# Reordering the pipelined steps of a gated-trace and attention kernel: out matmuls two lags ahead, moments two products ahead, three table steps earlier

## What is computed

```python
# block 1
ctx = causal_ema(x, tau_ctx)
gated = x * sigmoid(concat([x, ctx]) @ Wg.T + bg)
mod = 0.5 + sigmoid(gelu(x @ Wn1.T + bn1) @ Wn2.T + bn2)          # 32 channels
traces = [causal_ema(gated * mod[d], tau_raws[d]) for d in range(32)]
temporal = einsum('dbtc,dc->btc', traces, softmax(blend, axis=0))
gate = sigmoid(temporal @ Wtemp.T + btemp)
out = (gelu(x @ Wsoma.T + bsoma) * gate) @ Wout.T
x = x + (out - mean(out)) / sqrt(var(out) + 1e-5) * gamma + beta
# block 2: attention with 16 heads of 8; each row of the batch takes either the dense
# softmax with a prior bias, or the sparse one over 32 gathered neighbours, by its lam
Q, K, V = x @ Wq.T + bq, x @ Wk.T + bk, x @ Wv.T + bv
x = x + attention(Q, K, V, prior_mask, prior_indices, lam) @ Wo.T + bo
```

## Time and profile before

| what | us |
|---|---|
| median of 3 runs | 333.78 |
| lowest and highest of them | 333.19, 334.94 |
| the profiled execution, its own time | 332.17 |
| its span in the profile | 330.4 |

### The profile page before, as it was taken

How to read it: one execution, slowest core, us unless ns; L and a number is a source line. 1 busy time by engine, 2 the same in 40 slices (tenths; PEclk the granted TensorE clock), 3 DMA queues, 4 the chain that set the end, 5 groups by cost and what they waited for, 6 DMA issues and landing times. The chain is left out here.

```text
span 330.4 us, 9991 instructions
## 1 busy us (share of the span) xinstructions
PE 308.8 (93%) x3319; PEld 209.8 (64%) x3335; DVE 275.5 (83%) x1453; ACT 214.8 (65%) x458; POOL 246.6 (75%) x298
## 2 busy tenths in 40 slices
PE   8997888999999999999978898999999999999995
PEld 2554554746557375655535666878788778877873
DVE  3988898888969887796889666999999999999972
ACT  6763155555656646566446678778887887788863
POOL 3263586678686875665456966999999999999990
PEclk9999999999999999999999999999999999999999
DMA  6600021050412305013530435564444354301011
GB/s 187 211 2 26 7 67 32 16 129 3 111 34 59 86 0 145 1 35 66 77 51 2 82 94 86 82 133 127 129 102 117 87 129 100 72 7 30 5 34 32
DMA packets 29154, 23.07 MB, mean 70 GB/s; under 512 B 2736, under 2 KB 27824, under 8 KB 29104
## 3 DMA queue, kind: packets, MB, share of 16 engines
q1 hardware_dynamic: 29104, 22.44, 29.1%
HBM read 7.75 MB, written 2.10 MB: 30 GB/s over the span
## 5 line engine op out<-in xcount | busy, mean ns | idle before, releaser
L1596 POOL TENSOR_TENSOR arena<-arena,neg_max 128x512 f32<-128x512 f32 x128 | 129.6, 1042 | 14.1 <-DVE neg_max L1438 13.9
L1438 DVE CUSTOM_DVE_ANT_0 arena<-ps,arena 128x128 f32<-128x128 f32 x512 | 113.5, 286 | 11.5 <-PE ps L762 5.9
L1077 ACT ACTIVATE arena<-ps 128x512 f32<-128x512 f32 x128 | 69.6, 597 | 9.0 <-PE ps L776 9.0
L776 PE MATMUL ps<-ident_sb,arena 128*128 128x128 f32 x512 | 68.2, 276 | 0.0
L776 PEld LDWEIGHTS ps<-ident_sb,arena 128*128 128x128 f32 x512 | 56.4, 141 | 7.0 <-issue 4.3
L1515 POOL TENSOR_TENSOR arena<-arena 128x448 f32<-128x448 f32 (+6 forms) x56 | 42.8, 764 | 23.1 <-DVE arena L1269 19.7
L1438 DVE DVE_READ_ACCUMULATOR2_ANT neg_max<- 128x1 f32 x512 | 42.4, 83 | 0.0
L792 PE MATMUL ps<-arena 128*32 128x128 f32 x1024 | 41.2, 279 | 0.0
L1502 POOL TENSOR_TENSOR arena<-decay_a,arena 128x192 f32<-128x192 f32 x32 | 19.4, 636 | 21.8 <-ACT arena L921 21.8
L1269 DVE SCALAR_TENSOR_TENSOR arena<-ps,lag_c,arena 128x448 f32<-128x448 f32 (+6 forms) x56 | 25.7, 483 | 7.7 <-POOL arena L1515 7.0
L792 PEld LDWEIGHTS ps<-arena 128*32 128x32 f32 x1024 | 24.1, 109 | 6.9 <-issue 0.3
(11 more groups left out here) (169 smaller groups left out, 581.9 us busy)
## 6 DMA issues: line engine op xcount, KB each, us to landing
arena<-q_parts SPq DMA_DIRECT2D x96, 64.0 KB
arena<-k_parts SPq DMA_DIRECT2D x96, 64.0 KB
arena<-in_x SPq DMA_DIRECT2D x16, 256.0 KB, 3.4
arena<-in_xt SPq DMA_DIRECT2D x8, 256.0 KB, 2.8
out<-arena SPq DMA_DIRECT2D x7, 256.0 KB, 3.0
arena<-in_consts SPq DMA_DIRECT2D x1, 420.0 KB, 4.0
w_sb<-in_w SPq DMA_DIRECT2D x1, 384.0 KB, 6.2
w_sb<-in_w SPq DMA_DIRECT2D x1, 192.0 KB, 4.4
```

Of the source, the lines that this page charges most:

```text
L776: mm = pe.transpose(ps[1][:, q % 2, k * P:k * P + P], neg_t[q % NT_RING][:, k * P:k * P + P], ident)
L1077: act.activation(probT[q % PT_RING], ps[1][:, q % 2, :], ACT.Exp, scale=-1.0)\
L1438: dve.tensor_tensor_reduce(out=neg_t[q % NT_RING][:, cs], in0=ps[0][:, score_bank(c) + slot, cs], in1=nbias[n % 2], scale=1.0, scalar=3.0e ...
L1596: pool.tensor_tensor(t4, t4, neg_max[:, n % 2, 4 * z:4 * z + 4].unsqueeze(2).broadcast_to([P, 4, P]), ALU.subtract).then_inc(s["shifted"], 1)
```

## The change

Four things are moved; nothing is computed otherwise and no instruction is added or dropped.

1. On PE `b_out` (and the `c_less` ahead of it) stands behind lag 5 in place of lag 6, in all steps, and lags 6 and 7 come between `b_out` and `c_v`. Before, only lag 7 came behind `b_out`, and behind `c_v`.
2. On DVE `c_moments` stands behind product 5 in place of product 6, and products 6 and 7 come between it and `c_centre`. On POOL `c_rstd` moves the same way, ahead of the additions of lags 6 and 7.
3. `neighbours` goes from step 0, where it stood ahead of `c_moments`, to the end of `front`.
4. In step 0 `kept_bias` on DVE goes from ahead of `c_moments` to ahead of `b_temporal`, and `value_bias` on PE from behind `b_gate` to ahead of `b_cross`.

The core of the diff:

```diff
@@ tensor: step @@
                     f_gate_ctx(i, m + 1)
+                    value_bias()
                     b_cross(i, m)
...
                 b_gate(i, m)
-                if not closes:
-                    value_bias()
                 if closes:
                     c_less(i, m - 1, 1, 1)
                     c_less(i, m - 1, 0, 0)
-                f_lags(i, m + 1, range(4, 7))
+                f_lags(i, m + 1, range(4, 6))
                 if closes:
                     c_less(i, m - 1, 0, 1)
                 b_out(i, m)
+                f_lags(i, m + 1, range(6, Q))
                 if closes:
                     c_v(i, m - 1)
-                f_lags(i, m + 1, range(7, Q))
@@ vector: front and step @@
                 b_carries(i, m, NJ - 1, NJ)
+                neighbours()
...
+                if not closes:
+                    dve.wait_ge(s["const_ps"], 2)
+                    dve.wait_ge(s["rows_loaded"], 16)
+                    pro("kept_bias", dve.tensor_tensor(kept_bias[:], bank(1, 3)[:, 0:P], bo, ALU.add), waited=False)
                 b_temporal(i, m)
...
                 b_mixed(i, m)
-                f_lags(i, m + 1, range(4, 7))
-                if not closes:
-                    dve.wait_ge(s["const_ps"], 2)
-                    dve.wait_ge(s["rows_loaded"], 16)
-                    pro("kept_bias", dve.tensor_tensor(kept_bias[:], bank(1, 3)[:, 0:P], bo, ALU.add), waited=False)
-                    neighbours()
+                f_lags(i, m + 1, range(4, 6))
                 c_moments(i, m)
-                f_lags(i, m + 1, range(7, Q))
+                f_lags(i, m + 1, range(6, Q))
                 c_centre(i, m)
```

## The result

The changed kernel took 330.54 us (median of 10 runs, 329.62 to 331.27), the kernel before 333.12 (median of 10, 332.25 to 334.94; the three runs shown first had given 333.78). The ratio is 0.9919, with a 95% interval of 0.9901 to 0.9937: 2.6 us faster. I had forecast 332.1 and a range of 331.0 to 333.6. The direction was right, the size was not: the gain was 2.6 in place of 1.65. (One of six later executions of the changed kernel had a granted clock of about 0.75 from start to end and took 387.52 us; no table here uses it.)

The account below looks back on a forecast made before the run. In steps 2 to 5 PE and ACT set the pace; in step 1 DVE was late. The terms 1.2 + 0.15 + 0.3 = 1.65 us off 333.78 gave 332.1 us, range 331.0 to 333.6.

Parts of the forecast that it names:

- The blocks: Octet steps behind the pipeline: they keep their order, so a microsecond gained at the start is one at the end.
- The neighbour steps and the key bias at no cost: Front and step 0: 1.0 us and 0.28 us on DVE land in its pauses and cost nothing.
- a sign of being wrong: Step 0: an L572 that comes later than 30.1 us would show the prediction wrong.
- Step 0, out and moments: End of step 0: `b_out` and DVE's statistics start earlier, so the carries' product begins 1.21 us earlier.
- What is late next in step 1: Step 1, DVE's split of the modulation meeting POOL on the shared port: `b_cross` gains 1.2 us, ends 0.95 and 1.35.
- my rival of collisions: POOL wins the port and holds L1251, later steps lose 0.05 each: gain 1.0 us, 332.8 us, chance 0.13.
- Steps 1 to 5: Out and lags: the values' copy holds the carries, so 0.03 us a step, 0.15 for five; ends -0.1 and +0.2 a step.
- my sign of being wrong: Steps 2 to 5: a period that moves by 0.1 us or more either way would show the prediction wrong.
- Step 6: Copy of the values behind ACT's logarithm: it starts 0.3 us earlier and the gain passes on.
- The rival that the later steps gain too: If the copy's wait does not hold the carries, each later step gains: 2.6 us in all, 331.1 us, chance 0.12.
- The slower rival: PE's fp32 and bf16 changes cost about 0.24 us each, delaying `c_v` in six steps: 335.0 us, chance 0.08.
- The base: Whole kernel: the gain of 1.65 us was subtracted from a median of 333.78 us.

Follow-up runs that it names:

- the first four: Tables alone, reordering alone, PE's new order with tables, vector engines' new order with tables, against the kernel before: 0.62, 1.82, 2.43 and 0.18 us ahead.
- the next three: Changed kernel with two more matmuls ahead of `c_v` (0.01 us behind before), `c_v` ahead of both lags (4.20 ahead), POOL's beta addition earlier (step 1 18.74 us).
- both edits: Changed kernel with `c_v` ahead of both lags on PE and POOL's beta addition ahead of the inverse deviation: median 328.42 us, ratio to before 0.9859.
- the late-values kernel: Changed kernel with two more bf16 matmuls on PE between the lags and `c_v`: step period 19.75 us, 0.01 us behind the kernel before.
- `c_v` first: Changed kernel with `c_v` ahead of both lags on PE: 4.20 us ahead of the kernel before, ratio to it 0.9882.

## Why the prediction was wrong, point by point

The sum was 1.2 + 0.15 + 0.3 = 1.65, and the traces have 0.84 + 1.26 + 0.50 = 2.60. The term that failed is that of steps 1 to 5, 0.03 a step where 0.25 was measured.

- **The blocks.** Right: what the pipeline won moved the octet steps as a block, apart from the disturbances (shortest spans 2.6 apart, pipeline 2.60). The other kernels' shortest spans say the same, each 330.4 less its "ahead" to 0.1 us: 329.8, 328.6, 328.0 and 330.2 for the first four, 330.4, 326.3 and 327.2 for the next three, 325.6 for both edits.
- **The neighbour steps and the key bias at no cost.** Right. DVE's pause ahead of group 0's locals shrank from 1.33 to 0.59 us, and `b_cross` of step 0 did not wait longer for them: the PE pause ahead of it is 0.29 in place of 0.51. It stands at 30.45, past the 30.1 that I had named as a sign of being wrong, but so does everything in this execution; in the nine other traces with the tables in front it is at 30.11 to 30.15, in the two without at 30.10 and 30.14.
- **Step 0, out and moments: 1.21.** Nearly right. From `b_out`'s first matmul (37.57) to the statistics it was 1.17, not 1.09, and the carries' product was 1.10 earlier (41.92 less the 0.35 of this execution, against 42.67).
- **What is late next in step 1: 1.2, with 0.95 and 1.35 as ends.** Wrong by 0.36, and outside its ends. The mechanism stood as I wrote it, the size didn't: L1531 came 0.77 us earlier, not 1.04. Of the 0.27, 0.11 is the inverse deviation (1.36 earlier, not 1.47), the rest the addition of lag 6 behind it, which cost 0.60, not 0.43. And POOL won the second meeting (46.13 against 46.31), the half of my rival of collisions that came true; its other half, a loss in the later steps, didn't. In all twelve traces with the full clock in the pipeline L1245 (L1246 before) of step 1 ends 0.54 to 0.56 us behind POOL's L1531, though its row is between 1.27 and 1.75 long, while POOL's row keeps its 1.26 or 1.27. The 0.79 of step 2, which I took for the free time, is such a row too: it ends 0.54 behind POOL's 62.95 + 1.28; the late-values kernel has four steps without a meeting, and there the row takes 0.69. It goes the other way as well: the second instruction of POOL's L1501, at 46.69 beside L1250, took 1.04 where the others took 0.59 or 0.60. The Trainium skill (SBUF — State Buffer, "SBUF: two separate sides") calls the shared port an exclusive lock; these rows agree. I had used the rule for a sentence; with POOL's one addition out of the way the step got 0.65 shorter.
- **Steps 1 to 5: 0.03 a step.** The step that failed most: 0.25 a step, 1.26 in all in place of 0.15. The reasoning (the copy holds the carries, so count to `c_v`, not to `b_out`) was right; the kernels with `c_v` later and `c_v` first show it. The term was a difference of two sums of some three us, from the q part's end to the copy's start: 3.36 before, and 0.40 + 0.89 + 0.87 + 1.19 = 3.35 by my members after. It is 3.13, and I mis-sized two members: 0.40 from the q part's end to `b_out`'s first matmul, where it was 0.28 (56.03 to 56.31), and 1.19 from `c_v`'s first matmul to the copy, taken from the one row of before in which `c_v` had stood behind `b_out` in one run, where it was 1.09 (58.07 to 59.16). That is 0.22 of the 0.25. What makes the passes of `c_v` 0.10 shorter to the copy behind bf16 matmuls than behind `b_out`, no run isolates; in before its start, 58.68, is also just behind the end of ACT's third q part (57.94 + 0.69), for which it waits. My end of +0.2 a step was too near, and my sign of being wrong, a period that moves by 0.1 or more, came true.
- **Step 6: 0.3.** It was 0.50, about 0.2 as in every step and about 0.3 for the copy, which no longer stands behind the logarithm and its table load. The copy comes 9.32 us after `b_cross` of step 6 (155.76 - 146.44), as in every step, where it came 9.83 after it (158.02 - 148.19). The term left out the 0.2, as that of steps 1 to 5 did. The row of the copy, which now waits for PE alone:

```profile
155.76 0.60 ACT L946 ACTIVATE v_all<-ps 128x512 f32<-128x512 f32 x1 [0.34 <-PE ps L419]
```

- **The rival that the later steps gain too**, 2.6 us and 331.1, has the measured gain to the digit, and that is luck. Its condition was that the copy does not hold the carries, and the copy does. Its terms 1.2, 1.0 and 0.4 are off by +0.36, -0.26 and -0.10, which cancel.
- **The slower rival** (0.24 us for each change between fp32 and bf16, a price for which I had no row): wrong. In the changed kernel `b_out`, lags and `c_v` follow each other at 56.31, 57.20 and 58.07, with no gap.
- **The base.** I subtracted from 333.78, the median of three; of ten runs it is 333.12. With 2.60 off the one it would have been 331.2, inside the range; 0.66 of the miss of 1.56 is that, and I had seen that the profiled execution lay 1.6 below the median without asking why. The range was also narrower than my own terms: their far ends, 1.58, 1.0 and 0.4, add up to 2.98 and 330.8, not to the 331.3 that I wrote, and 2.60 lies within them.

## What to carry to other kernels

Follow a step's end to the last instruction on which the next step's first one waits, and move that one forward; here the values' product, behind which everything else had slack, gave nearly as much again when put first (1.60 us) as the whole reordering had given behind step 1 (1.76). A term that is the small difference of two long chains, times the number of steps, needs ends as wide as the error of both chains. A total that comes out right can hide terms that don't, so check a rival by its condition. And where DVE's instruction with two SBUF inputs meets one of POOL's, as L1245 does here, its end has to be worked out from POOL's (0.55 us behind it), not from DVE's own start.

## What I had not expected of the hardware

The granted clock fell for some 3.4 us in two traces and not in eight others, behind the same pause of 1.70 us, and cost 0.91 us in the profile of the changed kernel and 0.8 in that with `c_v` first (327.1 against its shortest, 326.3). The change between fp32 and bf16 matmuls in one row costs PE nothing that the traces show. A POOL row of four instructions let DVE in after the first of them: L1250, behind L1501 since 46.31, ended at 47.28, while L1501's row ran until 48.83.
